# A fused attention and soft mixture-of-experts layer: operations moved in the first and last attention groups and where the experts begin

## The reference

```python
q = gelu(x @ W1q + b1q) @ W2q + b2q          # k and v in the same way
scores = (q @ k.T) / sqrt(256 * 512) * tril  # no softmax
x = layernorm(x + layernorm(scores @ v) * ln_w + ln_b)

xn = layernorm(x) * gamma + beta
logits = (xn / norm(xn) * scale) @ (mu / norm(mu))     # 256 slots
dispatch = softmax(logits, over tokens)
combine = softmax(logits, over slots)
slot_in = dispatch.T @ xn
slot_out = gelu(slot_in @ w1 + b1) @ w2 + b2           # by expert
out = layernorm(x + combine @ slot_out)
```

## Time and profile before

| what | value |
|---|---|
| median of 3 runs | 583.03 us (583.0 to 583.11) |
| profiled execution, own time | 584.8 us |
| its span | 582.7 us |
| PE busy | 565.2 us (97%) |
| DVE busy | 489.7 us (84%) |
| POOL busy | 421.2 us (72%) |
| ACT busy | 406.9 us (70%) |

### The profile page before, as it was taken

The page is one execution under the profiler, slowest core; times in us unless marked ns, Lnnn a source line. Parts: engine busy times, 40 slices in busy tenths (PEclk is TensorE's granted clock), DMA queues, the critical chain, the costliest instruction groups (busy, mean ns, idle before and its releaser), DMA issues. The chain is left out here.

```text
span 582.7 us, 12013 instructions
## 1 busy us (share of the span) xinstructions
PE 565.2 (97%) x3892; PEld 525.7 (90%) x3892; DVE 489.7 (84%) x1052; ACT 406.9 (70%) x870; POOL 421.2 (72%) x406
## 2 busy tenths in 40 slices
PE   9999999999999999999999999989999999989992
PEld 7989989999899999999999989979999999978992
DVE  6579889899898889988989889998988777548996
ACT  4765666676767667766667676677679988754884
POOL 0869779798797787977979879785658777453553
PEclk9999999999999999999999999999999999999997
DMA  7424133042240422413304223024776777875965
GB/s 226 92 74 108 20 92 75 36 110 33 76 108 8 100 35 73 108 18 90 74 34 108 31 77 75 9 29 77 153 154 144 145 145 146 141 167 162 323 238 181
DMA packets 166930, 59.64 MB, mean 102 GB/s; under 512 B 139854, under 2 KB 159724, under 8 KB 166892
## 3 DMA queue, kind: packets, MB, share of 16 engines
q1 hardware_dynamic: 166608, 58.89, 43.3%
q10 hardware_dynamic: 284, 0.27, 0.1%
HBM read 27.68 MB, written 14.68 MB: 73 GB/s over the span
## 5 line engine op out<-in xcount | busy, mean ns | idle before, releaser
L529 POOL TENSOR_TENSOR h_lo<-xn_all,h_hi 128x512 fp32r<-128x512 f32 x32 | 41.6, 1301 | 68.0 <-ACT xn_all L645 67.0
L643 ACT ACTIVATE h_hi<-bank,bias_col 128x512 fp32r<-128x512 f32 x96 | 66.5, 692 | 18.7 <-PE bank L800 17.1
L798 PE MATMUL bank<-xnT_hi,w_hi 128*128 128x512 f32 x188 | 76.2, 405 | 0.0
L799 PE MATMUL bank<-xnT_lo,w_hi 128*128 128x512 f32 x188 | 74.4, 396 | 0.0
L800 PE MATMUL bank<-xnT_hi,w_lo 128*128 128x512 f32 x188 | 74.2, 395 | 0.0
L678 ACT CAST state_hi<-bank 128x512 fp32r<-128x512 f32 x57 | 33.6, 589 | 49.1 <-PE bank L933 49.1
L1702 PE MATMUL bank<-xn_all,e_tok 128*128 128x257 f32 x256 | 65.1, 379 | 0.0
L1197 DVE TENSOR_TENSOR state_lo<-bank,state_hi 128x512 fp32r<-128x512 f32 x57 | 39.4, 692 | 29.2 <-ACT state_hi L678 29.2
L1805 DVE STREAM_TRANSPOSE e_turn<-e_tok 128x256 f32<-128x256 f32 x64 | 40.1, 635 | 16.3 <-ACT e_tok L1587 14.8
L1587 ACT ACTIVATE e_tok<-bank,shift,xinv 128x256 f32<-128x256 f32 x64 | 36.2, 566 | 19.1 <-PE bank L1692 12.2
L1702 PEld LDWEIGHTS bank<-xn_all,e_tok 128*128 128x128 f32 x256 | 44.1, 189 | 3.8
(11 more groups left out here) (222 smaller groups left out, 2198.9 us busy)
## 6 DMA issues: line engine op xcount, KB each, us to landing
x_all<-in_L_attn_x SPq DMA_DIRECT2D x16, 512.0 KB, 4.1
kT<-k_turn SPq DMA_DIRECT2D x128, 64.0 KB, 2.5
ET_all<-e_turn SPq DMA_DIRECT2D x64, 128.0 KB, 4.0
xn_all<-in_xT SPq DMA_DIRECT2D x15, 512.0 KB, 4.7
out<-xn_all SPq DMA_DIRECT2D x15, 512.0 KB, 3.8
x_spill<-x_all SPq DMA_DIRECT2D x12, 512.0 KB, 2.9
ET_all<-x_spill SPq DMA_DIRECT2D x8, 512.0 KB, 5.2
w_sb<-in_L_ffn_w SPq DMA_DIRECT2D x2, 512.0 KB, 5.4
```

Source lines behind the costliest of these rows:

```text
L529: pool.tensor_tensor(h_lo[:, V_SLOT, m, :], hv[:, m, :], h_hi[:, V_SLOT, m, :].bitcast(F32), ALU.subtract).then_inc(hv_split, 1)
L643: nc.scalar.activation(h_hi[:, h_slot(j, n), m, :], ps, ACT.Gelu, bias=bias(n, m))
L798: nc.tensor.matmul(ps, w[0], xs[0], start=start, stop=False, skip_group_check=shared)
L799: nc.tensor.matmul(ps, w[0], xs[1], start=False, stop=False, skip_group_check=shared)
```

## The change

It moves operations in three places and computes the same.

In the opening group (g = 1): PE issues the second half of the scores ahead of `spread_mu_factors`; the first chunk's state update stays behind q's second hidden product, while the chunk itself goes behind v's first. ACT rounds the state between q's two halves (ahead of the second), DVE subtracts it ahead of q's first, and POOL makes the low part of the second sums of v ahead of hv's.

In the last two calls: DVE adds v's bias ahead of the statistics of the last pair; only the first sum of v is made in the call with projections, the second after the masking; `floor_norms` goes ahead of the state's first low part, and the two halves of `split_xnT` stand on both sides of the last one. ACT puts one of the norms behind the rounding of v's first half and the rounding of the first sums behind that of the state. POOL puts `invert_o` behind two low parts. PE adds the sums of v (`carry`) last, just ahead of `attend_chunk`.

At the experts: PE signals the first half of the last tile's fold by a semaphore of its own (`half_folded`), DVE divides half by half (in all batches), ACT loads the table of the gelu by a gelu over four columns ahead of the last `copy_slots`, and one of two `round_e` goes between the gelus.

```diff
@@ scalar, project=False @@
                         round_state(ba, i + 1, tail_hi[1])
+                        round_vsum(a, 0)
                         round_xnT(act, 0, 0)
...
@@ scalar, body @@
                     hidden(g, j, WQ1, 0)
+                    if attend and not settle:
+                        follow(0)
                     hidden(g, j, WQ1, 1)
-                    if attend:
+                    if attend and settle:
                         follow(0)
...
                     if not more:
-                        norms(act, 0, 0, (2, 3))
+                        norms(act, 0, 0, (2,))
                     round_v(g, 0)
+                    if not more:
+                        norms(act, 0, 0, (3,))
                     round_v(g, 1)
-                    if not more:
-                        round_vsum(g, 0)
...
@@ tensor, last_chunks @@
-                        carry(a, c, c % 2 == 0)
-                        read_state(ba, i + c, c, p, False, False, tail_hi[c], tail_lo[c])
+                        read_state(ba, i + c, c, p, c % 2 == 0, False, tail_hi[c], tail_lo[c])
 
                     def attend(c):
+                        carry(a, c, False)
                         attend_chunk(a, c, False, True).then_inc(chunk_done, 1)
...
@@ tensor, body @@
                     if opening:
+                        scores(a, (2, 3))
                         spread_mu_factors()
-                        scores(a, (2, 3))
                     hidden(g, j, WQ1, 1)
                     if opening:
                         pe.wait_ge(mu_copied, 1)
-                    if attend:
+                    if opening:
+                        update_state(a, 0, True)
+                    elif attend:
                         chunk(a, ja, ba, 0, p)
                     hidden(g, j, WV1, 0)
+                    if opening:
+                        chunk(a, ja, ba, 0, p, updated=True)
                     if attend:
                         chunk(a, ja, ba, 1, p)
...
@@ vector, last_body @@
+                    floor_norms(dve, 0, 0)
                     tail_state(1)
                     mask_scores(a)
+                    sum_v(a, ja, 1)
+                    tail_state(2)
                     sum_v(a, ja, 2)
-                    tail_state(2)
                     split_masked(a)
                     add_out(dve, a - 1, 2)
                     add_out(dve, a - 1, 3)
+                    split_xnT(dve, 0, 0, (0,))
                     tail_state(3)
-                    split_xnT(dve, 0, 0)
-                    floor_norms(dve, 0, 0)
+                    split_xnT(dve, 0, 0, (1,))
...
@@ scalar, experts @@
                     if last:
+                        act.wait_ge(n2_ready, GT * GROUPS + 1)
+                        nc.scalar.activation(square[:, 0, 0:4], square[:, 0, 0:4], ACT.Gelu)
                         copy_slots(b)
...
-                round_e(GROUPS - GB + 1)
-                round_e(GROUPS - GB + 2)
                 for half in range(2):
+                    round_e(GROUPS - GB + 1 + half)
                     act.wait_ge(hs_biased, 2 * half + 2)
...
@@ vector, normalise_slots @@
                     for s in range(SB):
+                        if b == B - 1 and s == 0:
+                            dve.wait_ge(half_folded, 1)
+                        elif b == B - 1:
+                            dve.wait_ge(tile_folded, TB * b + 2 * TB)
                         nc.vector.reciprocal(colinv[:, s:s + 1], fold_ps(b)[s][:, D:D + 1]).then_inc(colinv_ready, 1)
-                    for s in range(SB):
                         dve.wait_ge(colinv_ready, SB * b + s + 1)
```

More of the change, by code:

```diff
@@ L264, in round_xnT, with split_xnT @@
                 nc.scalar.copy(xnT_hi[q % 2][:, kb, :], xnT_ps[kb][:, :]).then_inc(xnT_rounded, 1)
-        def split_xnT(dve, k, q):
-            for kb in range(KB):
+        def split_xnT(dve, k, q, halves=range(KB)):
+            for kb in halves:
                 dve.wait_ge(xnT_rounded, KB * k + kb + 1)
@@ L601, in body @@
                     split_ktok(g, 0)
-                    if attend:
+                    if attend and more:
                         invert_o(pool, a, 1)
@@ L945, in carry, with chunk @@
                                      skip_group_check=True)
-                def chunk(a, ja, ba, c, p):
+                def chunk(a, ja, ba, c, p, updated=False):
                     i = GT * ja + c
-                    if i == 0:
+                    if i == 0 and not updated:
                         update_state(a, c, True)
@@ L1237, in body @@
                     if attend:
-                        follow(0)
+                        if settle:
+                            follow(0)
                         close_sum(a, ja)
@@ L1265, in body @@
                         follow(3)
+                        if not more:
+                            bias_v(g, j, 0)
                         pair_statistics(dve, a, 1)
@@ L1268, in body @@
                         floor_mu()
-                    bias_v(g, j, 0)
+                    if more:
+                        bias_v(g, j, 0)
+                    else:
+                        bias_v(g, j, 1)
                     if attend:
@@ L1272, in body @@
                         weight_out(a, 3)
+                    if not more:
+                        sum_v(g, j, 0)
+                        return
                     bias_v(g, j, 1)
                     if attend:
-                        if not more:
-                            sum_v(g, j, 0)
-                            sum_v(g, j, 1)
-                            return
                         add_out(dve, a, 2)
@@ L1703, in fold @@
                                                 xn[q][:, t % GT, :], start=(t == 0), stop=(t == TB - 1))
+                        if b == B - 1 and t == TB - 1 and s == 0:
+                            last.then_inc(half_folded, 1)
                     last.then_inc(tile_folded, 1)
```

9 lines of the change are left out of this document (6 added, 3 removed).

## The result

| | before | after |
|---|---|---|
| median, measured side by side | 583.07 us (582.66 to 585.64, 6 runs) | 578.99 us (578.07 to 581.37, 6 runs) |
| ratio of the times | | 0.9919, 95% interval 0.99 to 0.9938 |
| profiled execution, own time | 584.8 us | 581.37 us |
| its span | 582.7 us | 579.4 us |

What follows compares the result with a forecast made beforehand. TensorE (PE), busy 565.2 of 582.7 us, was taken to bound the kernel, leaving only its stalls to gain. Opening 1.7, last group 1.1 and experts 0.9 sum to 3.7 us: 583.03 - 3.7 = 579.3 us, range 578.4 to 580.9.

Steps and rivals of the forecast that it cites:

- the bracket plus 0.16 us: PE stalls: idle is counted from the drawn end, so each stall costs its bracketed idle time plus 0.16 us.
- the step from PE's 1.4 us to 1.1: Last attention group: PE alone gains 1.4 us, DVE's queue shortens by about 1 us, so 1.1 us was taken.
- Opening group: 1.7 forecast: Opening group: all four PE stalls go and weight loads shrink a little, 1.7 us; bounds 0.9 to 1.9.
- Last group: 1.1 forecast: Last attention group: first and third stalls go, second stays, two short new ones come; 1.1 us, bounds 0 to 1.5.
- after it the same 0.9 us: Last group: DVE's scaling ends near 394.5, and the next stage starts 0.9 us later, as before.
- Experts: 0.9 forecast: Experts' stage: 0.45 us from the half signal, 0.45 from table load and rounding; 0.9 together, between 0.4 and 1.1.
- leaves the chain: Experts' stage: the half signal moves the chain up 0.44 us and takes the second reciprocal (0.1) out; 0.45 us.
- I let it pass through whole: After each place: PE and DVE bind everything, so the summed 3.7 us reaches the kernel's time undiminished.
- DVE's queue deciding the last group: Last group, rival, chance 0.22: v's three sums each wait for POOL, next stage no sooner; 580.4 to 581.4 us.
- The opening giving only its first half: Opening group, rival, chance 0.12: stalls at 36.89 and 41.84 stay in other places, 0.5 to 0.8 less; 580.0 us.
- the rival: Routing stage, slower-kernel rival, chance 0.02: late DMA exchanges cost up to 1.1 us each, five of them; 584.8 us.
- The change doing little: Whole kernel, rival, chance 0.03: next stages take up what the places give back, within 0.2%; 582.5 us.

Runs made afterwards that it cites:

- e8: The whole change, but mu's factors again ahead of the scores' second half on PE; opening scores to last group 353.79 us, 0.55 more.
- e12: The whole change without the early table load and without the rounding between the gelus; last folds to first mixing product 14.53 us.
- e7: The whole change, but the second sum of v again right behind the first; last group 14.42 us, 1.97 more than with the change.
- e10: The whole change, with POOL's residual addition in the mixing waiting for DVE's negated mean of the group before; 581.17 us, ratio 0.9938.

## Why the prediction was too small

The direction, the three mechanisms and the absence of a cost on PE elsewhere were right. What failed are two steps of the sum: the price of a stall as "the bracket plus 0.16 us" (it was about 0.26), and in the last group the step from PE's 1.4 us to 1.1 because of DVE's queue (it gave 1.56). Every sign that it named in the changed profile is there, but for one: the next stage was to start at 393.7 and started at 393.23, in an execution whose opening began 0.3 us later, so 0.8 us early.

- **Opening group: 1.7 forecast, 1.97 measured.** The part of mu's factors and the weight loads around them was put at 0.5 in all and is 0.55 (e8). The step that failed is the price of a stall, "the bracket plus 0.16 us". Stalls at 34.14, 36.89 and 41.84 were put at 0.7 + 0.3 + 0.2 = 1.2 us; what is left of 1.97 without e8's part is 1.42. The matmul after a stall is itself followed late. These two rows of before follow the starts at 36.89 and 387.80:

```profile
37.12 0.28 PE L799 MATMUL bank<-state_lo,h_hi 128*128 128x256 f32 x1
...
388.02 0.28 PE L933 MATMUL bank<-v_lo,ktok_hi 128*128 128x256 f32 x1
```

They come 0.23 and 0.22 us behind them, where two matmuls of 256 columns otherwise start 0.12 us apart. So such a stall costs the bracket plus about 0.26 us, and the three of them (their followers come 0.20, 0.23 and 0.22 us behind) give the 0.2 us that was missing, within the rounding. I had taken the distance ahead of the stalled matmul only.

- **Last group: 1.1 forecast, 1.56 measured.** By PE the text had 1.2 + 1.1 - 0.3 - 0.6 = 1.4. From start to start, with the late follower, the first stall gave 1.3, the third 1.2, and the new ones took 0.5 each (0.46 and 0.51), which makes the measured 1.56 up to rounding. The two that went were each put 0.1 us too low. In the first the follower is not the reason: behind the scores it comes late without a stall too (382.66 behind 382.45 in after). There the update starts 0.81 us after the scores, whose end is drawn at 1.06, so the bracket is 0.25 short and not 0.16. The larger failure is the step from 1.4 to 1.1: "after it the same 0.9 us", which made DVE's end set the next stage. It did not before: the scaling ended at 395.57 and PE's last matmul (395.65 and 0.28 drawn) at 395.93, 0.53 ahead of the logits. The 0.9 us held 0.36 us of DVE waiting for PE. Counted from the transposes, DVE's end moved up by 1.24 us (13.13 to 11.89), more than the 1.0 forecast, and the slack took the rest: all but 0.04 of it is used up in after. The sums came out as reckoned, one stretched and two nearly free: 1.33 + 0.49 + 0.58 = 2.4 us instead of 2.31 + 0.93 = 3.2, so 0.8 of the 1.24. What the text had not seen is the small scaling of the variance (`ve_o`). It lasts 1.02 us in before and 0.20 in after. Both lie beside POOL's low part of k, here in before and then in after:

```profile
381.54 1.20 POOL L535 TENSOR_TENSOR ktok_lo<-xn_all,ktok_hi 128x512 fp32r<-128x512 f32 x1
...
381.74 1.02 DVE L144 TENSOR_SCALAR ve_o<-st_o 128x2 f32<-128x2 f32 x1
```

```profile
379.85 1.19 POOL L535 TENSOR_TENSOR ktok_lo<-xn_all,ktok_hi 128x512 fp32r<-128x512 f32 x1
```

Each time the scaling ends with it (382.76 by 382.74; 381.08 by 381.04), and in after only 0.16 us of it was left. One reading of the text was wrong without harm: POOL is not idle at 365.72, it runs operations of four columns there, one of them of 1.20 us from 365.86. The price of 1.05 us for two sums stands all the same, they take 1.07 us in the opening group (33.96) with POOL idle.

- **Experts: 0.9 forecast, 0.91 measured,** but by luck, as the right sum of wrong parts: 0.45 was put on each edit, and they gave 0.23 and 0.68 (e12). What "leaves the chain" on PE's side was only worth what ACT's queue could follow.

- **"I let it pass through whole".** Right up to the mixing (first mixing product 4.4 us sooner). In the mixing PE passes it on to its last matmul (4.41 us), but DVE, ACT and POOL end 9.0 to 11.4 us behind that by waits for stores and by the meeting of two small operations, which the forecast had not seen. The profiled pair shows 0.8 us against the change, the median pair of the first measurement 4.1 us, the lowest times 582.66 - 578.07 = 4.6, the pairs with an ordered or paused POOL 4.42 and 4.12. All agree with 4.44 by the marks to 0.4 us. The 4.7 of the ratio lies 0.3 above it, which the ratio's own interval covers. By the marks the time is 583.03 - 4.44 = 578.6 us, inside the range; the rest of the way to 578.3 is no step of the forecast.

- **The rivals.** DVE's queue deciding the last group (0.22) did not come, though e7 shows it real, 1.97 us by moving one sum. The opening giving only its first half did not come. In the routing stage DVE waited for one exchange, 0.2 us, and the stage took 113.07 us beside 113.04; in e10 it waited for two, 2.0 us in all and 1.6 at most, and the stage took 113.06. So such a wait need not cost the time that the rival put on it. The change doing little did not come.

The bounds were too tight for the same reason as the sum: the opening's 1.97 and the last group's 1.56 both lie above their upper ends, 1.9 and 1.5. The upper end of each term used the same price per stall, so the errors went one way, and an error in the unit price is not covered by adding bounds of the terms.

## What to carry to other kernels

Price a stall from start to start over the matmul before it and the one after it, not from the bracket: here some 0.26 us a stall lie outside the bracket, and with five stalls removed the tenth that was forgotten in each is half a microsecond. At a barrier, ask for each engine when it arrives, and count a gain up to the second-last arrival; an engine's distance to the next stage may hold waiting for another. When a stage that was not touched moves, set marks and compare stretches before judging by whole times.

## What was not expected of the hardware

- A DVE operation on four columns changes the pace of a stage: it lasts 0.16 us where it starts ahead of POOL's addition and 0.63 us where it starts 0.02 us behind it, and groups are 2.84 or 3.20 us apart. The mixing of one and the same program took 56.8 or 59.3 us; half of that difference is a wait for a store. When a store is late was not tried.
- Of two orders forced on it (wait: 59.4 to 59.7 us; pause: 57.9 to 58.8 us) none reaches the short rhythm throughout. Whether the meeting ends if one of the two inputs is taken out of SBUF was not tried.
- The same sum of 256 columns lasted 0.49, 1.33 and 2.34 us by what POOL did beside it. A scaling of two columns with one input in SBUF was held as well, 1.02 us where POOL's subtraction had just begun and 0.20 where it was about to end.
